# A fused two-layer kernel: skip term, mixer residual, modulation and gating scores of the second recurrence moved between engines

## The reference, cut to what matters

```
state = decay * state + dt_t[..., None] * b_t[:, None, :] * u_t[..., None]
y_t = jnp.sum(state * c_t[:, None, :], axis=-1) + D_param * u_t
y = y * _silu(zb);  mixer = y @ out_proj_w.T
x = x + ga * mixer
h = _layernorm(x) * (1 + cb) + sb
scores = sigmoid(h @ gate_w.T);  top 8 of (scores + expert_bias)
combine = 2.826 * selected scores / their sum
x = x + gb * (sum over 16 experts of combine * ((silu(h @ w_gate) * (h @ w_up)) @ w_down) + shared expert)
```

## Time and profile before

| | us |
|---|---|
| three runs | 712.29, 714.84, 715.96 |
| median | 714.84 |
| the profiled execution, time | 713.7 |
| the profiled execution, span | 711.8 |
| busy PE | 580.1 (81%) |
| busy DVE | 575.3 (81%) |
| busy ACT | 380.1 (53%) |
| busy POOL | 405.8 (57%) |
| recurrence, first scan to last scan | 302.09 to 544.36 |
| expert turns to the end | 544.4 to 711.8 |

### The profile page before, as it was taken

The page is one execution under the profiler, slowest core; times in us unless marked ns, Lnnn a source line. Parts: engine busy times, 40 slices in busy tenths (PEclk is TensorE's granted clock), DMA queues, the critical chain, the costliest instruction groups (busy, mean ns, idle before and its releaser), DMA issues.

```text
span 711.8 us, 6686 instructions
## 1 busy us (share of the span) xinstructions
PE 580.1 (81%) x1874; PEld 323.2 (45%) x1874; DVE 575.3 (81%) x744; ACT 380.1 (53%) x646; POOL 405.8 (57%) x344
## 2 busy tenths in 40 slices
PE   6597676578999888889878775777777997999997
PEld 3133232146668642233323232223324776778885
DVE  0765996734687769499999999999997894989795
ACT  4566110686613157866975663566564455565553
POOL 0005887343100020369899997979776653677776
PEclk9699666779899999689999998999999998999999
DMA  8000000600011000100000000000002331344340
GB/s 298 12 1 1 0 1 18 297 0 1 1 61 60 1 0 0 44 1 0 0 23 23 23 23 22 23 11 25 23 0 77 100 108 58 112 127 138 119 117 15
DMA packets 14596, 34.95 MB, mean 49 GB/s; under 512 B 1952, under 2 KB 2240, under 8 KB 14080
## 3 DMA queue, kind: packets, MB, share of 16 engines
q1 hardware_dynamic: 14560, 34.54, 14.9%
HBM read 33.33 MB, written 1.20 MB: 49 GB/s over the span
## 4 chain that ended last, share of the span: by engine, by line
PE 38%; DVE 25%; POOL 17%; issue 12%; ACT 7%; DMA 1%; POOLq 0%; DVEq 0%; SPq 0%; ACTq 0%
PE ps L940 18%; POOL arena L1728 16%; PE ps L617 5%; DVE arena L1646 4%; DVE arena L1416 3%; PE ps L891 2%; DVE arena L1623 2%; PE ps L780 2%; DVE ps L1400 2%; PE ps L747 2%; DVE ps L1575 1%; PE ps L828 1%; PE ps L843 1%; DVE place L1531 1%; PE ps L622 1%
## 5 line engine op out<-in xcount | busy, mean ns | idle before, releaser
L1728 POOL TENSOR_TENSOR arena<-arena 128x512 f32<-128x512 f32 x186 | 229.0, 1257 | 53.1 <-DVE arena L1646 37.2
L1646 DVE TENSOR_TENSOR_SCAN arena<-ps,carry,arena 128x512 f32<-128x512 f32 x128 | 156.3, 1261 | 0.3 <-ACT ps L1270 0.3
L1270 ACT ACTIVATE ps<-arena,abase 128x512 f32<-128x512 f32 x128 | 88.1, 691 | 88.2 <-DVE arena L1646 87.4
L1851 POOL TENSOR_TENSOR h_parts<-arena,h_parts 128x512 fp32r<-128x512 f32 x68 | 100.0, 1487 | 55.9 <-ACT h_parts L1304 53.2
L891 PE MATMUL ps<-arena,core 128*128 128x512 f32 x256 | 129.8, 632 | 0.0
L940 PE MATMUL ps<-x_parts,w_hi 128*128 128x512 f32 x272 | 100.7, 410 | 3.0 <-DVE arena L1646 2.5
L976 PE MATMUL ps<-bc,sel 96*128 96x512 bf16 x128 | 45.0, 411 | 53.8 <-DVE arena L1623 37.6
L1623 DVE TENSOR_TENSOR arena<-ps,arena 128x1024 f32<-128x1024 f32 x64 | 76.7, 1199 | 7.5 <-PE ps L976 7.5
L1721 DVE TENSOR_TENSOR arena<-arena 128x512 f32<-128x512 f32 x64 | 72.5, 1132 | 2.2
L891 PEld LDWEIGHTS ps<-arena,core 128*128 128x128 f32 x256 | 51.9, 203 | 41.0 <-issue 30.2
L1716 DVE TENSOR_TENSOR arena<-ps,arena 128x512 f32<-128x512 f32 x68 | 46.4, 682 | 26.4 <-PE ps L940 20.1
(11 more groups left out here) (225 smaller groups left out, 984.3 us busy)
## 6 DMA issues: line engine op xcount, KB each, us to landing
arena<-weight_rows SPq DMA_DIRECT2D x64, 256.0 KB, 3.3
arena<-in_wB SPq DMA_DIRECT2D x2, 2048.0 KB, 12.4
arena<-in_wD SPq DMA_DIRECT2D x8, 384.0 KB, 3.1
arena<-in_cstB SPq DMA_DIRECT2D x1, 1368.0 KB, 5.7
x<-in_x SPq DMA_DIRECT2D x4, 256.0 KB, 4.9
arena<-slot_rows SPq DMA_DIRECT2D x4, 256.0 KB, 3.7
arena<-scale_rows SPq DMA_DIRECT2D x4, 256.0 KB, 3.8
out_x<-x SPq DMA_DIRECT2D x4, 256.0 KB, 2.2
```

The costliest lines, as they stand in the source:

```text
L1270: A(bank(6 + c), ch(DTG[:, c, :], i), ACT.Exp, scale=ABASE[:, c * NS + n:c * NS + n + 1]).then_inc(*done(f"dec{n}_{c}", i))
L1646: nc.vector.tensor_tensor_scan(ST[:, k % ST_RING, :], bank(6 + c), DBU[:, (2 * q + c) % DBU_RING, :], CARRY[:, k:k + 1], ALU.mult, ALU.add ...
L1728: mul = lambda o, a, b: nc.gpsimd.tensor_tensor(o, a, b, ALU.mult)
L1851: nc.gpsimd.tensor_tensor(HWP[:, 1, q % 4, :], (HW if e < E1 else HH)[:, q % H_RING, :], HWP[:, 0, q % 4, :].bitcast(f32), ALU.subtract).t ...
```

## The change

- **Skip as a diagonal product.** ACT writes two diagonal matrices of D (`diag`, turn 1). PE adds `D * u` into the y banks by one more matmul for each c ahead of `y0` (`Du0`, `Du1`). `skip` leaves DVE. For chunks 0 to 2 ACT copies y from PSUM (`y_copy`, two copies) and POOL gates it as before; for chunk 3 DVE gates directly from PSUM.
- **Residual off DVE.** For chunks 0 to 2 ACT scales the mixer's output into SBUF (`gam`), PE centres x and this in one accumulated group (two matmuls where one stood), and POOL adds it to x. Chunk 3 keeps it on DVE.
- **Modulation.** `modF` is an ACT instruction, and `x_hi` an ACT step of its own.
- **Gating scores in PSUM.** Router output, exponentials and scores stay in PSUM banks; the "+ 1" ahead of the reciprocal goes from DVE (`g_one`, L1659) to ACT. DVE keeps the other steps.
- **Turns.** The side steps come earlier, and the gating of chunk 0 starts at turn 28 (34 before), of chunk 1 at m = 1, all four parts together (m = 5 to 8 before), of chunk 2 at m = 6, of chunk 3 at m = 20.
- **The end of the recurrence.** The last y sums stand earlier between the first expert products, and the first up product later.

```diff
-SIDE = {"pe": {9: ["m_out"], 11: ["centreF"], 13: ["varF"], 15: ["g_router"]},
-        "act": {11: ["sqF"], 12: ["lnF", "rsF"], 14: ["g_act", "x_hi"]},
-        "dve": {4: ["skip_0", "skip_1"], 8: ["x_mamba"], 12: ["normF", "modF"]},
-        "pool": {5: ["gated_0", "gated_1"], 15: ["x_lo"]}}
...
+SIDE_AT = {
+    "pe": by_turn(chain("pe", [(6, "m_out"), (8, "centreF"), (10, "varF"), (13, "g_router")]),
...
+    "act": by_turn([(1, "diag", 0)], chain("act", [(3, "y_copy"), (6, "gam"), (8, "sqF"), (10, "rsF"), (11, "modF"), (12, "x_hi"), (13, "g_act")]),
...
+    "dve": by_turn(chain("dve", [(9, "normF")]), [(NQ + 5, "gated", LAST), (NQ + 9, "x_mamba", LAST), (NQ + 15, "normF", LAST)],
+                   [(start + k // pace, f"gating{k}", i) for i, (start, pace) in enumerate(((28, 1), (NQ + 1, 4), (NQ + 6, 1), (NQ + 20, 1))) for k in range(4)]),
+    "pool": by_turn(chain("pool", [(2, "gated"), (7, "x_mamba"), (12, "x_lo")]), [(NQ + 20, "x_lo", LAST)]),
+}
...
+                    if n == 0:
+                        mm(bank(c + 2 * (i % 2)), DIAG(c), ch(U[:, c, :], i), start=True, stop=False).then_inc(*done(f"Du{c}", i))
...
             def centre_f(i):
...
+                if i < LAST:
+                    pe.wait_ge(*upto("gam", i))
+                    mm(b, CORE_("centre"), ch(X, i), start=True, stop=False)
+                    mm(b, CORE_("centre"), GAM(i), start=False, stop=True).then_inc(*done("centreF", i))
...
+            gate_product(0)
+            y_sum(NQ - LAG)
+            gate_product(1)
+            y_sum(NQ - LAG + 1)
+            up_product(0)
+            for m in range(1, TURNS + LAG_E):
                 side_work(NQ + m)
+                if 1 < m < TURNS:
+                    gate_product(m)
                 if m < TURNS:
-                    expert_turn(m)
-                if m < LAG:
-                    y_sum(NQ + m - LAG)
+                    up_product(m)
+                if m < LAG - 1:
+                    y_sum(NQ + m + 1 - LAG)
...
+            def gam(i):
+                act.wait_ge(*upto("m_out", i))
+                A(GAM(i), bank(2 * (i % 2)), ACT.Copy, scale=modcol(1, GA)).then_inc(*done("gam", i))
...
+            def mod_f(i):
+                act.wait_ge(*upto("normF", i))
+                A(ch(HD, i), ch(HD, i), ACT.Identity, scale=modcol(1, CB), bias=modcol(1, SB_)).then_inc(*done("modF", i))
...
-            def skip(i):
-
-                for c in range(DI):
-                    dve.wait_ge(*upto(f"y{NS - 1}_{c}", i))
-                    stt(ch(U[:, c, :], i), ch(U[:, c, :], i), col(f"D{c}"), bank(c + 2 * (i % 2)), ALU.mult, ALU.add).then_inc(*done(f"skip_{c}", i))
...
             def gate_score(i):
-                dve.wait_ge(*upto("g_act", i))
-                if i < NCH - 1:
-                    ts(scores(i, 1), scores(i, 0), 1.0, None, ALU.add).then_inc(*done("g_one", i))
+                if i < LAST:
                     dve.wait_ge(*upto("g_one", i))
                     nc.vector.reciprocal(scores(i, 0), scores(i, 1)).then_inc(*done("g_score", i))
...
+            def x_mamba(i):
+                pool.wait_ge(*upto("centreF", i))
+                nc.gpsimd.tensor_tensor(ch(X, i), GAM(i), ch(X, i), ALU.add).then_inc(*done("x_mamba", i))
```

More of the change, by code:

```diff
@@ L11 @@
+import itertools
 from contextlib import ExitStack
@@ L53, in side_steps @@
[L53 to L65, removed]
+LAST = NCH - 1
@@ new lines, with chain, by_turn @@
+SIDE_STEPS = {"y_copy": ["y_copy_0", "y_copy_1"], "gated": ["gated_0", "gated_1"], "rsF": ["lnF", "rsF"], "diag": ["diag_0", "diag_1"], "turned": ["g_turned"]}
+def chain(engine, names, first=NS):
+    return [((i + 1) * first + at, name, i) for i in range(LAST) for at, name in names if (engine, name, i) not in (("pe", "g_router", 1), ("act", "g_act", 1))]
+def by_turn(*parts):
+    table = {}
+    for q, name, i in sorted(itertools.chain(*parts), key=lambda item: item[0]):
+        table.setdefault(q, []).append((name, i))
+    return table
@@ L66, with side_names @@
+def side_names(name, i):
+    if name.startswith("gating"):
+        return G_LAST if name[-1] == "0" and i == LAST else G_STEPS[int(name[-1])]
+    if name == "g_act" and i < LAST:
+        return ["g_act", "g_one"]
+    return SIDE_STEPS.get(name, [name])
+TURN_BANK = (2, 3, 1, 1)
+GATE_BANK = (1, 0, 1, 3)
 TAKEN = -2.7182817e38
@@ L293, in sequences @@
         side_add("dve", q)
-        if q in GATE_AT:
-            j, part = GATE_AT[q]
-            dve += [(step, j) for step in G_STEPS[part] if step != "g_score" or j < NCH - 1]
         side_add("pool", q)
@@ L525, in build, with gate_bank, scores @@
         hd_bank = lambda i: 2 * (i % 2)
+        def gate_bank(i, lo, hi):
+            return bank(GATE_BANK[i])[:, lo:hi]
+        def scores(i, k):
+            return gate_bank(i, 64 * k, 64 * (k + 1))
         def ch(buf, i, off=0):
@@ L1281, in turned @@
                 A(WT[i], bank(TURN_BANK[i], 0, E1), ACT.Copy).then_inc(*done("g_turned", i))
+            side = {"diag": diag, "y_copy": y_copy, "gam": gam, "sqF": sq_f, "rsF": rs_f, "modF": mod_f, "g_act": g_act, "x_hi": x_hi, "turned": turned}
             def side_work(q):
@@ L1632, in norm_f, with gated @@
                 tt(ch(HD, i), bank(2 * (i % 2) + 1), ch(TF, i), ALU.mult).then_inc(*done("normF", i))
-                dve.wait_ge(*upto("normF", i))
-                ts(ch(HD, i), ch(HD, i), modcol(1, CB), modcol(1, SB_), ALU.mult, ALU.add).then_inc(*done("modF", i))
-            side = (skip, x_mamba, norm_f)
+            def gated(i):
+                for c in range(DI):
+                    dve.wait_ge(*upto(f"y{NS - 1}_{c}", i))
+                    tt(ch(U[:, c, :], i), bank(c + 2 * (i % 2)), ch(Z[:, c, :], i), ALU.mult).then_inc(*done(f"gated_{c}", i))
             dbu(0)
```

156 lines of the change are left out of this document (88 added, 68 removed).

## The result

The changed kernel takes 701.66 us (median of four runs, 700.98 to 706.94); the kernel before, run beside it, 713.57. The ratio is 0.9851, 95% interval 0.9816 to 0.9886: faster by 1.5%. So the sign and most of the mechanism held, and the gain came out larger than the sum: 11.9 us by the medians (8.1 to 13.1 by the interval), where the sum said 8.1. The profiled execution took 701.9 us (span 700.1) against 713.7 (711.8), 11.8 us less.

The account below looks back on a forecast made before the run. DVE was taken to bound the recurrence, PE the first expert turns. Gains of 2.9 + 3.1 + 2.1 = 8.1 us off 713.7 gave 705.6, adjusted to 706; own range 702 to 710, 8-in-10 range 700 to 713.

Parts of the forecast that it names:

- recurrence, net: Recurrence: 13.5 us leaving DVE, less new waits of 7.6, 1.3 and 1.7, gains 2.9 us.
- waits at `normF`: Recurrence, chunks 0 to 2: DVE stands for `rsF` from ACT, 3.4, 2.1 and 2.1 us, together 7.6 lost.
- wait at the first reciprocal: Gating of chunk 0: DVE arrives before ACT's exponential and sum behind turn 29's decays, 1.3 us lost.
- `Du` of chunk 0: PE's turn 4: four more records of diagonal products, for which DVE waits, 1.7 us lost.
- residual, three: Recurrence: three residuals leave DVE at 0.72 us less some 0.08 of overlap, 1.9 us gained.
- PE late at a later `dbu`: Later chunks: extra `Du` and centring products on PE cost nothing; without its cover, 1 us for each of three chunks.
- first expert turns: PE fills the 2.52 us hole with ready y sums, plus 0.6 for a slow y sum: 3.1 us gained.
- root of chunk 3 and behind: PE's 4.29 us hole at the router shrinks by one turn of products, 2.1 us gained.
- "a us ahead": Recurrence: PE makes the next turn's spread more than a us ahead, so its added products cost nothing.
- The first: Rival: gains behind the recurrence don't come, DVE limits turns 1 to 9; 711 to 712 us, chance 0.2.
- the second: Rival: new waits in the recurrence are free because POOL is full in turns 16 to 33; 700 to 702, chance 0.15.
- The third: Rival: POOL's lag makes the variance and `rsF` a turn late at three places; 720 to 722 us, chance 0.1.

Follow-up runs that it names:

- norm10: Changed kernel with `normF` of chunks 0 to 2 one turn later on DVE; 693.54 us, ratio 0.971 to the kernel before.
- skip_dve: Changed kernel with the skip of chunks 0 to 2 back on DVE, without their diagonal products; 701.85 us, ratio 0.984 to the kernel before.
- resid_dve: Changed kernel with the mixer residual of chunks 0 to 2 back on DVE, one turn ahead of the centring; 711.07 us, ratio 0.997 to the kernel before.
- old_y_order: Changed kernel with the last y sums and first expert products on PE in the old order; 705.92 us, ratio 0.991 to the kernel before.
- before_exp_psum: Kernel before with only chunk 0's gating exponential written to PSUM, so `g_one` reads PSUM; 711.04 us, ratio 0.997 to the kernel before.
- after_again: The changed kernel itself run a second time, as its control; 699.82 us, ratio 0.982 to the kernel before.
- norm10_gate29_du3: norm10 plus chunk 0's gating one turn later on DVE and its diagonal products in PE's turn 3; 688.84 us, ratio 0.964 to the kernel before.
- router16: Changed kernel with the router of chunk 3 one expert turn earlier on PE (16 instead of 17); 704.47 us, ratio 0.986 to the kernel before.
- mod_dve: Changed kernel with `modF` of all four chunks back on DVE, directly behind `normF`; 708.57 us, ratio 0.993 to the kernel before.

## Why the prediction was right, and where its sizes were off

| step | predicted | measured |
|---|---|---|
| recurrence, net | 2.9 | 3.2 |
| waits at `normF` | 3.4, 2.1, 2.1 | 3.42, 2.03, 2.03; worth 7.5 to 8.1 (norm10) |
| wait at the first reciprocal | 1.3 | 1.20 |
| `Du` of chunk 0 | 1.7 | 1.65 |
| skip less `Du` of chunk 0 | 2.2 | 1.6 (skip_dve, one profile) |
| residual, three | 1.9 | 2.4 (resid_dve, waits taken off) |
| PE late at a later `dbu` | 0 | 1.42 |
| gating in PSUM beyond `g_one` | 0 | 0.8 gained |
| first expert turns | 3.1 | 4.0 (3.9 by old_y_order) |
| root of chunk 3 and behind | 2.1 | 4.7 (2.0 between before_exp_psum and after_again) |

**The recurrence.** The base was that DVE is full, so that what leaves it is gained and what it waits is lost. It held to a few tenths in norm10, in norm10_gate29_du3 and in skip_dve. With DVE's waits of over 0.15 us taken off, the stage went from 238.9 to 224.5, 14.3 us of work less where the sum has 13.5, and the waits from 2.2 to 13.3, 11.1 more where it has 10.6: both sides came out, and 3.2 is their difference. The waits were worked out from which scan frees which bank, and each came within 0.1 us. The two terms that I had put at nothing cancel in part. The 1.42 at 453.64 is PE coming late: it had stood for 0.77 and 1.04 us, and its next y sum took 3.58 us for four records against 1.88 at full clock:

```profile
448.09 3.58 PE L927 MATMUL ps<-arena,core 128*128 128x512 f32 x4
```

The granted clock of these 3.4 us was 0.50, that is 1.2 GHz. So the cover that I named, "a us ahead", is used up when PE falls to 1.2 GHz just ahead of a longer side step. It is not in every profile: router16 and norm10 have the same two stops of 0.77 and 1.04 us, the y sum behind them took 1.88, and DVE had no wait there. mod_dve and skip_dve show the 1.42 in chunk 0 instead. On the other side the last gating steps, which I held at the same length, took 0.21 and 0.22 us with a PSUM operand against 0.34 and 0.72 (before, at 446.86 and 447.70); with the selection's 0.20 against 0.33 that is 0.8.

**`g_one`.** The 4.96 us did leave DVE, but the working ascribed them to one instruction. before_exp_psum shows that taking the stall from it alone hands most of it to the next one. The whole is gained in the changed kernel, where the selection, the picking and the weighting (L1736, L1749, L1755) read one input from PSUM, which I had costed at nothing. That this is the reason is argued from the selection, which stood 3.27 us in before_exp_psum and here takes 0.20 beside a running product of POOL:

```profile
415.22 3.72 POOL L1796 TENSOR_TENSOR arena<-arena 128x512 f32<-128x512 f32 x3
415.30 0.20 DVE L1736 TENSOR_TENSOR arena<-ps,wC 128x64 f32<-128x64 f32 x1
```

The rule of the Trainium skill that I had weighed ("SBUF — State Buffer", "Who interferes with whom") gives at most 1.8, by the length of one POOL instruction (0.7 by the one then running, which ended at 428.98). The stage of before_exp_psum comes near it, yet by another way: `g_one` and the selection behind it each stood across several POOL instructions, whereas most DVE steps of these traces were let go behind one, as that rule has it. The same section says that an instruction of VectorE with at most one SBUF input, outside the two-port modes, doesn't contend; the selection's 0.20 against 3.27 agrees. `g_one` and `modF` have one SBUF input and stood all the same (4.93, 4.31), so by that rule they must run in such a mode; no run here shows the mode itself.

**The first expert turns.** The hole was named rightly; its size was put at 2.52 + 0.6 and measured 3.9. What I left out is that the first up product ran slowly as well: in the old order two of its matmuls start 0.43 us apart (538.39, 538.82), at full clock 0.23.

**The root of chunk 3.** This is the term of the sum that was most off in size. The hole fell by 2.43 (4.29 to 1.86), close to the 2.1. But in these two profiles the products behind it are slow for a time, and that time is shorter in the second. Before, the second of these rows is still slow 4.4 us after the first; after the change the products are fast again from 588.27 on:

```profile
599.81 0.77 PE L940 MATMUL ps<-x_parts,w_hi 128*128 128x512 f32 x1
...
604.22 0.63 PE L940 MATMUL ps<-x_parts,wD 128*128 128x512 f32 x1
```

```profile
584.86 0.77 PE L985 MATMUL ps<-x_parts,w_hi 128*128 128x512 f32 x1
587.57 0.63 PE L985 MATMUL ps<-h_parts,w_hi 128*128 128x512 f32 x1
588.27 0.39 PE L985 MATMUL ps<-h_parts,w_hi 128*128 128x512 f32 x1
```

From the router's start to the end of the slow stretch it is 7.1 us before (598.08 to 605.16) and 4.4 after: with the router itself (1.89, 1.18) some 1.5 us of lost time are saved (0.7 in the router, 0.2 for each of four to five slow products). Hole and clock make 3.9 of the 4.7; the rest is within the 1.2 us between two profiles. The forecast priced a hole by its length alone.

The 1.5 us belong to this pair of profiles and not to the length of the hole. before_exp_psum has the hole of before, and its products are fast again 4.4 us after the restart, not 7.1. old_y_order has the hole of the changed kernel, and its products are fast at once. First two rows of the one, then two of the other:

```profile
596.02 1.06 PE L912 MATMUL ps<-wC,arena 128*128 128x16 f32 x8 [4.28 <-DVE arena L1634]
600.43 0.40 PE L940 MATMUL ps<-h_parts,w_hi 128*128 128x512 f32 x1
```

```profile
585.44 1.07 PE L955 MATMUL ps<-wC,arena 128*128 128x16 f32 x8 [1.86 <-ACT arena L1309]
586.67 0.40 PE L983 MATMUL ps<-x_parts,wD 128*128 128x512 f32 x1
```

Of the seven profiles with a hole of 1.86 or 1.87 us at the router, three have a slow stretch behind it (the changed kernel, its control, norm10) and four have none. So this stage gained between 2.0 and 4.7 us, depending on which profiles are set side by side, and the forecast's 2.1 lies at the lower end.

**The rivals.** The first (gains that don't come, 711 to 712) is refuted by the last two stages: the first expert turns gained 3.9 or more and the root at least 2.0; the second (free waits) by norm10, though its time was the nearer one: the right number for the wrong reason. The third, a slower kernel through POOL's lag, didn't occur; no wait of DVE in the recurrence was released by POOL.

## What to carry to other kernels

When a step is moved to another engine, work out whether its input is ready at its new place: here two table entries, `normF` one turn ahead of the root and the router one turn too near to it, cost some 10 us, nearly as much as the whole change brought (12). On a full engine price a wait as its full length; on PE slow products behind it can come on top. They came in some profiles and not in others, so a single pair of profiles can overstate or understate a gain, here by 1.5 us. An instruction that seems ten times too long may be a stall that the next of its kind inherits: change the operands of the kind, not the one instruction.

## What the runs showed of the hardware

- DVE instructions with all inputs in SBUF stood while POOL's products ran, for very different times. Four stood until several POOL instructions in a row had ended: 4.93 for 0.18 us of work, 3.27 for 0.33, 4.31 and 3.05 for 0.55. Others were let go behind the one that was running, with the next already begun (0.33 at 437.31, 1.27 at 573.70 in the kernel before). With the input, or one of two, in PSUM the same steps took 0.20 and 0.81 us beside such products. The replacements of found values (`MATCH_REPLACE8`, 128x16) took their 0.16 us beside a running POOL instruction, and the reciprocal of before_exp_psum (L1661, at 427.83) its usual 0.55.
- What PE's clock did behind a stop was not fixed by the length of the stop. From the router's start, PE's products were slow for 7.1 us after 4.29 us of waiting (mean granted clock 0.53) and for 4.4 us after 4.28; after 1.86 us they were slow for 4.4 us in one profile (0.61) and at full speed in another (1.00).
